# Building the expert routing list backwards: one-hot matmuls and per-tile gathers in place of 32 scatters

## The reference

```
x = layernorm(x + attention(x, Wq, Wk, Wv, Wo, betas))
x = layernorm(x + retention(x, ctx, ctx, xWq, xWk, xWv))
x = layernorm(x + ffn(x, Wg, bg, W1, b1, W2, b2))

def ffn(x, Wg, bg, W1, b1, W2, b2):            # 8 experts, hidden width 512, top-1 gate
    gate_scores = softmax(einsum('btd,de->bte', x, Wg) + bg)
    top1_idx    = argmax(gate_scores)
    top1_mask   = one_hot(top1_idx, 8)
    top1_weight = sum(gate_scores * top1_mask, keepdims=True)
    h = silu(einsum('btd,edh->bteh', x, W1) + b1)
    o = einsum('bteh,ehd->bted', h, W2) + b2
    return sum(o * top1_mask[..., None], axis=2) * top1_weight
```

## Time and profile before

| | |
|---|---|
| median of 3 runs | 901.7 us (901.68 to 901.89) |
| the profiled execution's own time | 903.15 us |
| its span, first to last instruction | 901.3 us |
| PE busy over the span | 712.1 us (79%) |
| POOL busy over the span | 513.4 us (57%) |
| retention block | about 601.8 to 684.8 us of the span |
| gate block | 684.8 to 771.0 us |
| expert block | 771.0 to 869.7 us |
| finish block | 869.7 to the end |

### The profile page before, as it was taken

How to read it: one execution, slowest core, us unless ns; L and a number is a source line. 1 busy time by engine, 2 the same in 40 slices (tenths; PEclk the granted TensorE clock), 3 DMA queues, 4 the chain that set the end, 5 groups by cost and what they waited for, 6 DMA issues and landing times. The chain is left out here.

```text
span 901.3 us, 26782 instructions
## 1 busy us (share of the span) xinstructions
PE 712.1 (79%) x9501; PEld 597.7 (66%) x9502; DVE 605.1 (67%) x1217; ACT 528.7 (59%) x1119; POOL 513.4 (57%) x524
## 2 busy tenths in 40 slices
PE   4789999999999999999999999748994600599920
PEld 3577788788778778778778877645664500598920
DVE  4378788788788788878878878745885510244438
ACT  3677787788788778778778878321221100477720
POOL 2167667757757756766765775633431167266742
PEclk8799999999999999999999999967996555699975
DMA  7567767767667677676776776611093011400033
GB/s 239 117 179 200 187 170 205 176 163 215 171 161 216 172 172 199 178 183 177 197 180 170 209 171 162 160 32 36 25 284 51 0 39 53 124 32 29 32 108 93
DMA packets 122154, 127.72 MB, mean 142 GB/s; under 512 B 7424, under 2 KB 101920, under 8 KB 118032
## 3 DMA queue, kind: packets, MB, share of 16 engines
q1 hardware_dynamic: 119584, 122.17, 52.8%
q0 software_dynamic: 2544, 5.21, 1.7%
HBM read 67.42 MB, written 43.16 MB: 123 GB/s over the span
## 5 line engine op out<-in xcount | busy, mean ns | idle before, releaser
L328 POOL TENSOR_TENSOR lhs<-pos_qv,ungate 64x1024 f32<-64x1024 f32 x64 | 151.7, 2370 | 161.9 <-PE mix L495 151.2
L614 ACT ACTIVATE psT<-bank 128x512 f32<-128x512 f32 x128 | 72.6, 594 | 92.5 <-PE bank L484 92.5
L766 DVE TENSOR_TENSOR lhs<-mix,zg_all 64x512 f32<-64x512 f32 x128 | 88.2, 689 | 5.8 <-PE mix L467 1.9
L353 POOL TENSOR_TENSOR e_qk<-e_qk 128x512 f32<-128x512 f32 (+2 forms) x96 | 78.6, 819 | 20.1 <-DVE e_qk L707 15.1
L484 PE MATMUL bank<-const,ps 128*128 128x128 f32 x512 | 70.0, 280 | 21.7 <-POOL ps L343 21.5
L598 ACT ACTIVATE e_qk<-e_qk 128x512 f32<-128x512 f32 x128 | 82.3, 643 | 0.0
L721 DVE TENSOR_REDUCE s_max<-bank 128x8 f32<-128x512 f32 x64 | 44.2, 691 | 48.7 <-PE bank L453 47.8
L467 PEld LDWEIGHTS mix<-pos_qv 64*64 64x64 f32 (+1 forms) x2048 | 65.6, 137 | 13.7 <-issue 11.2
L484 PEld LDWEIGHTS bank<-const,ps 128*128 128x128 f32 x512 | 55.2, 142 | 27.9 <-issue 15.7
L574 ACT ACTIVATE qk_tok<-bank 128x512 f32<-128x512 f32 x128 | 73.2, 601 | 0.0
L603 ACT ACTIVATE qkT<-bank 128x512 f32<-128x512 f32 x128 | 71.2, 610 | 1.8 <-PE bank L430 1.0
(11 more groups left out here) (212 smaller groups left out, 1694.5 us busy)
## 6 DMA issues: line engine op xcount, KB each, us to landing
scratch_qv<-qv_out SPq DMA_DIRECT2D x32, 1024.0 KB, 5.7
pos_qv<-scratch_qv SPq DMA_DIRECT2D x64, 512.0 KB, 6.6
swapT<-qkT SPq DMA_DIRECT2D x64, 256.0 KB, 4.0
zg_all<-scratch_z SPq DMA_DIRECT2D x64, 256.0 KB, 3.8
sorted_x<-padding SPq DMA_DIRECT2D x1, 2515.5 KB, 18.5
r_all<-in_x_dram SPq DMA_DIRECT2D x4, 512.0 KB, 7.0
cx<-in_ctx_dram SPq DMA_DIRECT2D x8, 256.0 KB, 2.7
w<-in_L_ffn_W_dram SPq DMA_DIRECT2D x1, 2048.0 KB, 9.7
```

The source lines that it names most:

```text
L328: pool.tensor_tensor(lhs[0:L, 1 - n, :, :], pos_qv[s, :, DK:], ungate[s, :, :], ALU.mult).then_inc(vg_ready, 1)
L353: pool.tensor_tensor(dst, e_qk[:, 0:c, DK:], e_qk[:, c:2 * c, DK:], ALU.add).then_inc(k_summed, 1)
L614: act.activation(psT[:, 4 * f:4 * f + 4, :], turn_bank[f % 2][:, :].rearrange("p (h s) -> p h s", h=4), ACT.Copy).then_inc(psT_evac, 1)
L766: dve.tensor_tensor(dst, mix[odd * DK:(odd + 1) * DK, g, :].rearrange("p (i n k) -> p i n k", n=SEG, i=4), zg_all[odd * DK:(odd + 1) * DK, ...
```

## The change

It replaces the scatter of x2 into a sorted DRAM tensor and its loading back by an inverse list: for each tile row, which token stands there. Then each tile's rows are gathered from a plain copy of x2.

- The tensor `sorted_x`, the tile `padding`, its fill, its 2.5 MB store and the four loads of `xs` are gone.
- In the gate block SP stores `x2_row` as it is to `x2_rows` (one direct DMA) when x2 and `top` are there. Its last column now holds `top` (written by ACT, not read from there).
- After `place`, DVE splits it into tile number and row in the tile (shift and mask, two casts back to float), makes `in_row` [128, 32, 128] and `in_tile` [128, 32, 39] by comparisons with constants; POOL multiplies `in_tile` by token number plus one, in two halves; PE adds up 32 matmuls `in_row`ᵀ x `in_tile` in one bank, which then holds token number plus one for each tile row and 0 for an empty one. Four DVE operations make `token_of` (where to read) and `row_to` (where to write).
- In the expert block POOL's list is written out in full: 39 gathers (12 of them ahead of the first scatter, the others in fours between fours of scatters) and 39 scatters. A gather's landing is told to ACT by `publish`: POOL waits for the transfer and runs a tiny memset that raises `gathered`. `y` has a slot for each tile, so the waits for its reuse go. The other engines keep their loop over two tiles.

```diff
 # retention_phase
-            pool.memset(padding[:, :, :], 0.0).then_inc(padded, 1)
-            pool.wait_ge(padded, 1)
-            pool.tensor_copy(padding[:, :, D:].rearrange("p t o -> p (t o)"), cst("spare_row")).then_inc(padded, 1)
...
-            sp.wait_ge(padded, 2)
-            sp.dma_start(sorted_x.rearrange("(t p) d -> p t d", p=P), padding[:, :, :]).then_inc(preloaded, 16)
-            sp.wait_ge(preloaded, 16 * (len(preload) + 1))
+            sp.wait_ge(preloaded, 16 * len(preload))
 # gate_phase, SP
+            sp.wait_ge(x2_kept, NG)
+            sp.wait_ge(top_kept, 1)
+            sp.dma_start(x2_rows.rearrange("(b p) d -> p b d", p=P), x2_row[:, :, :]).then_inc(x2_stored, 16)
+            sp.wait_ge(x2_stored, 16)
 # gate_phase, PE
+            for b in range(B):
+                if b % G == 0:
+                    pe.wait_ge(in_row_ready, b // G + 1)
+                if b % (B // 2) == 0:
+                    pe.wait_ge(in_tile_ready, b // (B // 2) + 1)
+                last = pe.matmul(list_bank[:, 0:NT], in_row[:, b, :], in_tile[:, b, :], start=(b == 0), stop=(b == B - 1))
+            last.then_inc(listed, 1)
 # gate_phase, POOL
-            pool.tensor_copy(x2_row[:, :, D:].rearrange("p b o -> p (b o)"), cst("token_row")).then_inc(x2_kept, 1)
-            pool.wait_ge(x2_kept, NG + 1)
-            pool.wait_ge(placed, 1)
-            for b in range(B):
-                pool.indirect_dma_start(sorted_x, bass.IndirectOffsetOnAxis(ap=place[:, b:b + 1], axis=0),
-                                        x2_row[:, b, :], None).then_inc(scattered, 16)
-            pool.wait_ge(scattered, 16 * B)
+            for i in range(2):
+                half_b = slice(i * B // 2, (i + 1) * B // 2)
+                dims = [P, B // 2, NT]
+                pool.wait_ge(placed, i + 1)
+                pool.tensor_tensor(in_tile[:, half_b, :], in_tile[:, half_b, :],
+                                   cst("token_row")[:, half_b].unsqueeze(2).to_broadcast(dims), ALU.mult).then_inc(in_tile_ready, 1)
 # gate_phase, DVE
+            dve.tensor_scalar(tile_u[:, :], place[:, :], 7, None, ALU.logical_shift_right).then_inc(done, 1)
+            dve.tensor_scalar(row_u[:, :], place[:, :], P - 1, None, ALU.bitwise_and).then_inc(done, 1)
...
+            for g in range(NG):
+                if g % (NG // 2) == 0:
+                    s = slice(G * g, G * g + B // 2)
+                    dims = [P, B // 2, NT]
+                    dve.tensor_tensor(in_tile[:, s, :], cst("tile_at").unsqueeze(1).to_broadcast(dims),
+                                      tile_f[:, s].unsqueeze(2).to_broadcast(dims), ALU.is_equal).then_inc(placed, 1)
+                s = slice(G * g, G * g + G)
+                dve.tensor_tensor(in_row[:, s, :], cst("lane").unsqueeze(1).to_broadcast([P, G, P]),
+                                  row_f[:, s].unsqueeze(2).to_broadcast([P, G, P]), ALU.is_equal).then_inc(in_row_ready, 1)
+            dve.wait_ge(listed, 1)
+            dve.tensor_scalar(token_of[:, :], list_bank[:, 0:NT], -1.0, 0.0, ALU.add, ALU.max)
...
 # expert_phase, SP
-            for i, ready in enumerate(x_loaded):
-                a, z = cuts[i], cuts[i + 1]
-                sp.dma_start(xs[:, a:z, :], rows[:, a:z, :]).then_inc(ready, 16)
 # expert_phase, POOL
+            def gather(t):
+                pool.indirect_dma_start(xs[:, t, :], None, x2_rows,
+                                        bass.IndirectOffsetOnAxis(ap=token_of[:, t:t + 1], axis=0)).then_inc(x_loaded[t % (AHEAD + G)], 16)
+            def publish(a, z):
+                for t in range(a, z):
+                    pool.wait_ge(x_loaded[t % (AHEAD + G)], 16 * (t // (AHEAD + G) + 1))
+                pool.memset(mark[:, a:z], 0.0).then_inc(gathered, z - a)
+            def scatter(t):
+                pool.wait_ge(y_added, t + 1)
+                pool.indirect_dma_start(y_rows, bass.IndirectOffsetOnAxis(ap=row_to[:, t:t + 1], axis=0),
+                                        y[:, t, :], None).then_inc(stored, 16)
+            for t in range(AHEAD):
+                gather(t)
+                if t > 1:
+                    publish(t - 2, t - 1)
+            publish(AHEAD - 2, AHEAD)
+            for t in range(0, NT, G):
+                ahead = t + AHEAD
+                for i in range(ahead, min(ahead + G, NT)):
+                    gather(i)
+                for i in range(t, min(t + G, NT)):
+                    scatter(i)
+                if ahead < NT:
+                    publish(ahead, min(ahead + G, NT))
+                if ahead < NT <= ahead + G:
+                    pool.memset(xs[:, NT:, :], 0.0).then_inc(gathered, 1)
+            pool.wait_ge(stored, 16 * NT)
 # expert_phase, ACT (stage_x)
+                act.wait_ge(gathered, t + 1)
```

More of the change, by code:

```diff
@@ L1059, in gate_phase @@
         row_of, place_f = sb("row_of", [P, B, E]), sb("place_f", [P, B])
-        place = ctx.enter_context(nc.sbuf_tensor("place", [P, B], U32))
+        place, tile_u, row_u = (ctx.enter_context(nc.sbuf_tensor(n, [P, B], U32)) for n in ("place", "tile_u", "row_u"))
+        tile_f, row_f = sb("tile_f", [P, B]), sb("row_f", [P, B])
+        in_row, in_tile = sb("in_row", [P, B, P]), sb("in_tile", [P, B, NT])
+        empty = sb("empty", [P, NT])
+        list_bank = ctx.enter_context(nc.psum_tensor("list_bank", [P, BANK], F32))
         b1_bank = ctx.enter_context(nc.psum_tensor("b1_bank", [P, BANK], F32))
@@ L1126, in _ @@
             act.activation(ex[:, :, :], logits[:, :, :], ACT.Exp).then_inc(exp_done, 1)
+            act.wait_ge(top_ready, 1)
+            act.activation(x2_row[:, :, D:].rearrange("p b o -> p (b o)"), top[:, :], ACT.Copy).then_inc(top_kept, 1)
         @block.gpsimd
@@ L1284, in expert_of @@
             return eng.value_load(tile_expert[0:1, bass.ds(t, 1)], min_val=0, max_val=E - 1)
-        @block.sync
-        def _(sp):
-            rows = sorted_x.rearrange("(t p) d -> p t d", p=P)
-            for i, ready in enumerate(x_loaded):
-                a, z = cuts[i], cuts[i + 1]
-                sp.dma_start(xs[:, a:z, :], rows[:, a:z, :]).then_inc(ready, 16)
         @block.gpsimd
         def _(pool):
-            pool.memset(xs[:, NT:NT + 1, :], 0.0).then_inc(pad_done, 1)
-            pool.wait_ge(pad_done, 1)
-            pool.wait_ge(x_loaded[0], 16)
-            def step(half, p, one, two):
-                t = 2 * half + p
-                if two:
-                    u, q = t - 1, 1 - p
-                    if is_step(t, 3):
-                        for ready in x_loaded[1:]:
-                            pool.wait_ge(ready, 16)
-                    if not is_step(t, 1, 2):
-                        pool.wait_ge(stored[q], 16 * (half if p == 1 else half - 1))
-                    pool.tensor_copy(row[q][:, :], xs[:, bass.ds(u, 1), D:].rearrange("p o d -> p (o d)")).then_inc(row_ready, 1)
-                    pool.wait_ge(row_ready, u + 1)
-                    pool.wait_ge(y_added, u + 1)
-                    pool.tensor_tensor(carrier[:, :], xs[:, NT, 0:1], xs[:, NT, 1:2], ALU.add)
-                    pool.indirect_dma_start(y_rows, bass.IndirectOffsetOnAxis(ap=row[q][:, :], axis=0),
-                                            y[q][:, :], None).then_inc(stored[q], 16)
-            run_steps(pool, step, NT, peeled=2)
-            pool.wait_ge(stored[0], 16 * ((NT + 1) // 2))
-            pool.wait_ge(stored[1], 16 * (NT // 2))
@@ L1400, in step @@
                         stage_b(t + 1, 1 - p)
-            run_steps(act, step, NT)
+            run_steps(act, step, NT, peeled=1)
         @block.vector
@@ L1422, in step @@
                 if one:
-                    if is_step(t, NT - 1):
-                        dve.wait_ge(hid, 2 * t)
-                    else:
+                    if not is_step(t, NT - 1):
                         stage_w1(t + 1, 1 - p)
```

84 lines of the change are left out of this document (43 added, 41 removed).

## The result

The changed kernel takes 921.07 us (median of 4 runs, 919.30 to 924.95) against 901.69 for the kernel before on the same chip. The ratio is 1.0226, 95% interval 1.0188 to 1.0264. It is slower by 19.4 us, where 20.3 less were forecast. The profiled execution took 924.95 us, with a span of 923.1.

What follows compares the result with a forecast made beforehand. It saw stalls around `padding`, POOL's scatters at the gate block's end and PE in the expert block as limits, with POOL limiting the latter afterwards: -2.3 - 4.0 - 27.2 + 13.2 = -20.3 us, median 881.4, range 869 to 896.

Steps and rivals of the forecast that it cites:

- Fill removed, 2.3: Retention's start: without the fill of `padding`, PE's second transposes come 2.3 us sooner; bounds 1.1 and 3.4.
- Store removed, 4.0: Border from retention to gate block: without the store of `padding` only a barrier is left, 4.0 us gained.
- List, 27.2: Gate block's end: the inverse list replaces 32 scatters, so the expert block starts 27.2 us earlier.
- Store of x2: Gate block: the 2.1 MB store takes 15 us, hidden behind the list's matmuls; up to 15 us if uncovered.
- POOL's price of a gather: Expert block: a gather takes POOL as long as a scatter, 971 ns plus 0.30 gap, 1.27 us each.
- the rival with the dear gather: Expert block: a gather costs more than a scatter, break-even 1.79 us each; 906 us at 1.9. Chance 0.10.
- the one in which `w_cur` copies hold POOL: Expert block: each of 39 copies holds POOL for its whole length, 17 us in place of 3.3; 895 us. Chance 0.12.
- the 3.3 us of my term: Expert block: DVE's `w_cur` copies slow some of POOL's DMA starts, 3.3 us in all; bounds 0 and 10.
- From then PE needs 2.1 a tile: Expert block: after the first tile PE needs 2.1 us each, POOL feeds one per 2.6 and ends the block.
- "slower" a small chance: Whole kernel: chance 0.10 of being slower than before; 0.88 was given to faster, 0.02 to the same.
- The border behind the block: Expert block to finish: profiled from 864.79, the last scatter's issue end, to 869.70; no term for a change.
- its signs of being wrong: Mostly expert block: gather over 1.2 us, POOL gaps over 0.4, landing waits, PE at low clock, or a 3 us border.

Runs made afterwards that it cites:

- e12: Kernel before with padding's fill moved to ScalarE at the gate block's start and its store issued from that block: 894.71 us, ratio 0.9946.
- e8: e3 plus two unused work chains beside the gathers (80 rounds TensorE-VectorE, 80 ScalarE copies), as a probe: 959.44 us.
- e2: Changed kernel with each of the 39 gathers made a plain load of 128 whole rows, unsorted: 873.31 us, ratio 0.9698.
- e13: Changed kernel with the 39 scatters made plain stores, output rows at the wrong tokens: 898.70 us, ratio 0.9959.
- e15: e13 with a 400-element fill and its wait on GpSimd behind each gather: 876.71 us, ratio 0.9725.
- e9: e8 with plain loads for the gathers, then 39 scatters back to back before the tiles, 110 rounds: 983.11 us.
- e5: Changed kernel with gathers still indirect but reading rows in order, not an expert's tokens: 917.52 us, ratio 1.0183.
- e1: Changed kernel with stored and gathered rows 512 bytes wide instead of 516: 922.15 us, ratio 1.0241.
- e4: Changed kernel with every tile's expert the constant 3, so no expert number is loaded: 908.52 us, ratio 1.0052.
- e10: e8 with each gather issued only after the one before has landed, 110 rounds: 986.44 us.
- e14: e8 with a 400-element fill and its wait on GpSimd behind each gather, gathers 1.67 us apart: 934.05 us.
- e16: Changed kernel with a 400-element fill and its wait on GpSimd behind each gather and each scatter: 917.61 us, ratio 1.0191.
- e6: Changed kernel with 4 gathers ahead instead of 12, then one gather, one scatter, one publish in turn: 912.58 us, ratio 1.0126.
- e17: Changed kernel with a 400-element fill and its wait on GpSimd behind each gather only: 911.93 us, ratio 1.0119.
- e3: Changed kernel with all 39 gathers issued and landed before the first tile, then scatters alone: 919.81 us, ratio 1.0215.
- e11: Kernel before with padding's fill on ScalarE behind the gate block's exponential and its store issued from there: 901.61 us, ratio 1.0006.

## Why the prediction was wrong

By its steps, in the profiled spans:
- *Fill removed, 2.3*: held. From the block's first operation to TensorE's second transposes 5.4 us in place of 7.7.
- *Store removed, 4.0*: held. The border is 0.31 us. Retention as a whole went from 83.0 to 75.8 us, 7.2 less in place of 6.3; in e12, whose only change is that both moved to the gate block, it took 76.0.
- *List, 27.2*: held to 0.2. 64 records in 13.85 us (14.4 forecast), at the low clock; the border behind it was the short one. POOL's product took 1.61 (1.3 forecast); an `in_row` took 0.68 (0.65 forecast), but 1.72 the two that ran beside a product of POOL, hidden but for a few tenths.
- *Store of x2*: hidden, 13.5 us from 707.9, over before the list.
- *POOL's price of a gather*: held, 973 ns; the rival with the dear gather is out. So is the one in which `w_cur` copies hold POOL: 78 indirect DMAs cost 76.0 us, 78 x 0.974, so even the 3.3 us of my term weren't there. The Trainium skill's rule for it (SBUF — State Buffer, "Who interferes with whom") adds that issue order decides; the 78 DMAs here show nothing of the 17 us.
- ***"From then PE needs 2.1 a tile", with the sum of POOL as the block's length: this step failed.*** 107.0 us were forecast from the block's start to the last scatter. It took 145.0 (from 737.8, which is 18.7 behind `place` at 719.17, to 882.85). I had priced an indirect DMA by the time that POOL is busy issuing it, and taken the other engines as unaffected. What the runs showed in its place: with indirect DMAs 1.26 to 1.3 us apart, results of TensorE reach the other engines up to 6 us late (in e8 ScalarE's updates are late as well), and a tile takes 3.7 us on average over the block, not 2.1. From the first gather to the last scatter's end the changed kernel took 144.7 us; with plain loads (e2) it was 97.5, with plain stores 122.3 (e13), with plain stores and spaced gathers 99.9 (e15). The trace of before could not show this: its 32 scatters at 1.27 us ran while nothing else did, and in its tile loop no two were closer than 1.62 us. The forecast had given "slower" a small chance, but by a dearer gather; what made it slower was none of its rivals.
- *The border behind the block*, taken as unchanged, cost 3.2 us more. It is POOL's end-of-block step, which the trace records as a drain: 2.67 us behind 32 DMAs of POOL and 3.23 behind 39 in the kernel before, 6.44 behind 78 here. e2 and e13, where half of the 78 are plain, have 6.44 too, so it is the number and not the kind. It is not in proportion: e9's 117 had 7.66, and the gate block's own is still 1.71 without any.

The sum: -7.2 (retention) - 27.2 (list) + 51.2 (block, 145.0 for 93.8) + 3.2 + 1.3 (attention block, nothing to do with the change) + 0.5 (finish) = 21.8, and the spans differ by 923.1 - 901.3 = 21.8.

What is shown: the holds come from indirect DMAs (e2, against e5, e1, e4), of both kinds (e9, e13), not from gathers in flight as such (e10) but from how closely they follow one another. None at 1.67 us or more in the probe and in the tile loop (e14, e15, e16), nor in the kernel before, whose closest are 1.62 apart; holds at 1.26 (the changed kernel, e8, e9, e13), and where three gaps of 1.28 to 1.5 stand in a row (e6). Each probe was free again 54.0 us (e8) and 54.8 (e9) after the first of its 39 was issued, 6 us after the last. If a backlog is what holds, 54 / 39 = 1.4 us for each is an estimate of what it costs to clear. That it is so simple is not shown: the packets of e8's gathers kept up at 1.26, and in e13 a group of four could leave a backlog of half a microsecond by this figure, while its holds are 2 to 4 us. No arrangement that I ran and that computes all of the reference brings the changed kernel under the one before: e17's 1.0119 and e6's 1.0126 are the nearest.

What stays open: what in an indirect DMA makes the updates of TensorE and ScalarE wait and not VectorE's, GpSimd's issuing or what follows it; and why the hold begins after nine in a row in the first twelve of the changed kernel, after two to four later in the loop, and in the probe e8 after twelve for ScalarE and nineteen for TensorE. One rival was not tested: that the recording of the profile takes part. In the probes the trace loses semaphore events together with the holds: of the 624 with which 39 transfers land it has 56 for e8's gathers and 90 for e9's scatters, but 610 in e14, 624 in e10, and all 624 for e9's plain loads, 0.52 us apart. In the tile loop events are missing without holds too (e16 has 316 of its gathers' 624), so this settles nothing.

The lower clock that follows the holds (0.78 in the window) can be bounded. The prediction had named it among its signs of being wrong. The whole block, before and after:
```profile
771.00:864.80 93.80, 82.76 (x664) 78.45 (x664) 36.77 (x118) 66.21 (x236) 57.30 (x118) 0.94 0.19 54
```
```profile
737.85:882.85 145.00, 99.50 (x664) 95.19 (x664) 38.49 (x118) 67.48 (x236) 78.27 (x97) 0.81 0.14 35
```
The same 664 matmul records took 16.7 us more of TensorE's time at the lower mean clock. So at most about a third of the 51.2 us is the clock; how much of that third lengthened the block is not shown.

## What to carry to other kernels

Price an indirect DMA not by its issue on GpSimd alone but by how soon the next one follows. Where TensorE or ScalarE feeds other engines, try them 1.7 us apart, even by giving GpSimd something else to do, as long as GpSimd doesn't become the limit: it paid in e15 and e17, but e16, which spaces the scatters too, is 6 us slower than e17. Running them all where nothing else works (e3) gained nothing here. When waits name an engine whose rows had long ended ("remote"), look at what is in flight at that moment instead of at the engine. A removed stall is only worth its length if the work that caused it finds a place with slack: e12 issues a store 25 us earlier in the gate block than e11, and its scatters start 6.3 us sooner behind `place`.

## What the runs showed of the hardware

- In e8's held stretch the recorded semaphore events of ScalarE and TensorE came at steps of 0.70 us: ScalarE's copies 0.70, 1.40 or 2.09 apart, TensorE's rounds at 2.80, while VectorE's updates were seen within 0.06 us.
- A busy TensorE row is no proof of a result: its updates came up to 6.0 us after the recorded end.
- More work on GpSimd made the kernel faster, 22 us in e15 against e13 and 9 in e17 against the changed kernel.
- The end of a block costs more the more DMAs GpSimd issued in it, plain ones too: 2.67 us for 32, 3.23 for 39, 6.44 for 78, 7.66 for 117.
